# Two graph attention layers on one core: the first phase's pipeline is shortened by a step and put in another order

## The reference

```python
# graph attention, layer 0: h = x @ W; s1 = h @ a1; s2 = h @ a2
e = leaky_relu(s1[:, None] + s2[None, :], 0.2)
out0 = elu(softmax(where(adj > 0, e, NEG_INF), axis=1) @ h)
# attention, layer 1: q, k, v = x @ Wq.T + bq, x @ Wk.T + bk, x @ Wv.T + bv
scores = where(adj > 0, q @ k.T / sqrt(128), NEG_INF)
out1 = elu(softmax(scores, axis=-1) @ v)
# together
h = maximum(layernorm(x), 0); x = x + out0(h, adj)
h = maximum(layernorm(x), 0); x = x + out1(h, adj)
```

## Time and profile before

| what | us |
|---|---|
| median of 3 runs | 1703.05 (1699.79 to 1706.76) |
| the profiled execution, as timed | 1698.98 |
| its span in the profile | 1697.2 |
| DVE busy | 1220.4 (72%) |
| PE busy | 1195.3 (70%) |
| POOL busy | 1131.2 (67%) |
| ACT busy | 928.7 (55%) |

### The profile page before, as it was taken

How to read it: one execution, slowest core, us unless ns; L and a number is a source line. 1 busy time by engine, 2 the same in 40 slices (tenths; PEclk the granted TensorE clock), 3 DMA queues, 4 the chain that set the end, 5 groups by cost and what they waited for, 6 DMA issues and landing times.

```text
span 1697.2 us, 23466 instructions
## 1 busy us (share of the span) xinstructions
PE 1195.3 (70%) x5503; PEld 944.0 (56%) x5554; DVE 1220.4 (72%) x6625; ACT 928.7 (55%) x1891; POOL 1131.2 (67%) x1206
## 2 busy tenths in 40 slices
PE   2667877877877778777765566766776676767676
PEld 1344555555555555555545456665766666666665
DVE  3567888888888888888888366656665665566565
ACT  2769888888878878888852222332233323332322
POOL 1237766766766666666666477777777777777773
PEclk9878777777777778777775566567566666566665
DMA  9869999999999999999922122222222222222221
GB/s 293 347 238 394 399 401 400 392 384 378 378 385 380 385 381 386 369 388 386 378 59 56 50 58 57 66 65 65 64 66 66 65 63 66 64 66 64 66 65 41
DMA packets 113049, 368.10 MB, mean 217 GB/s; under 512 B 33553, under 2 KB 58642, under 8 KB 80146
## 3 DMA queue, kind: packets, MB, share of 16 engines
q1 hardware_dynamic: 66242, 285.50, 43.6%
q0 software_dynamic: 38464, 81.08, 17.4%
q10 hardware_dynamic: 8208, 0.03, 0.3%
HBM read 353.80 MB, written 12.72 MB: 216 GB/s over the span
## 4 chain that ended last, share of the span: by engine, by line
POOL 33%; DVE 27%; PE 20%; issue 13%; ACT 4%; DMA 2%; SPq 1%; POOLq 0%; ACTq 0%; DVEq 0%
POOL arena L598 32%; PE psum L1443 6%; PE psum L1429 4%; PE psum L1415 4%; ACT arena L1175 3%; PE psum L1382 3%; DVE arena L754 2%; DVE arena L757 2%; DMA table<-arena 1%; DVE arena L880 1%; DVE arena L864 1%; DVE arena L875 1%; DVE arena L892 1%; DVE arena L889 1%; DVE arena L827 1%
## 5 line engine op out<-in xcount | busy, mean ns | idle before, releaser
L568 POOL DMA_INDIRECT arena<-table,arena x576 | 553.8, 961 | 260.2 <-issue 160.6
L598 POOL DMA_INDIRECT arena<-table,arena x576 | 549.0, 953 | 184.0 <-issue 174.9
L1175 ACT ACTIVATE arena<-arena 128x2048 bf16<-128x2048 int32 x256 | 484.8, 1894 | 26.0 <-DMA arena<-in_adj_dram 26.0
L1382 PE MATMUL psum<-arena 128*128 128x512 bf16 x973 | 283.7, 428 | 51.5 <-ACT arena L1175 46.8
L864 DVE SCALAR_TENSOR_TENSOR arena<-arena 128x131 f32<-128x131 f32 (+1 forms) x768 | 267.0, 348 | 15.1
L1429 PE MATMUL psum<-arena 128*128 128x131 f32 (+1 forms) x768 | 200.6, 433 | 103.8 <-ACT arena L1317 102.1
L1415 PE MATMUL psum<-arena 128*128 128x18 f32 x768 | 145.1, 322 | 166.1 <-DVE arena L827 165.7
L1415 PEld LDWEIGHTS psum<-arena 128*128 128x128 f32 x768 | 138.4, 265 | 185.0 <-DVE arena L827 184.7
L1429 PEld LDWEIGHTS psum<-arena 128*128 128x128 f32 x768 | 179.1, 329 | 107.5 <-issue 107.5
L1382 PEld LDWEIGHTS psum<-arena 128*128 128x128 bf16 x1024 | 110.0, 116 | 189.0 <-issue 67.4
L1422 PE MATMUL psum<-arena 128*128 128x1 f32 x768 | 134.7, 291 | 108.0 <-DVE arena L847 108.0
(11 more groups left out here) (205 smaller groups left out, 2089.3 us busy)
## 6 DMA issues: line engine op xcount, KB each, us to landing
arena<-in_adj_dram SPq DMA_DIRECT2D x256, 1024.0 KB, 12.2
arena<-table,arena POOLq DMA_INDIRECT x1152
table<-arena POOLq DMA_DIRECT2D x32, 132.0 KB, 4.5
table<-arena SPq DMA_DIRECT2D x16, 256.0 KB, 9.6
arena<-table SPq DMA_DIRECT2D x64, 64.0 KB, 1.9
out_dram<-arena SPq DMA_DIRECT2D x16, 256.0 KB, 2.4
arena<-in_x_dram SPq DMA_DIRECT2D x4, 0.5 KB, 12.2
arena<-in_L_gnn_W_dram SPq DMA_DIRECT2D x1, 64.0 KB
```

The lines of the kernel that those rows point to most:

```text
L568: pool.indirect_dma_start(Gt[:, v % GROUP, c + 1, :], None, table0, bass.IndirectOffsetOnAxis(idx_now[:, v % GROUP, c:c + 1], 0))\
L598: pool.indirect_dma_start(Gt[:, t % GROUP, c + 1, 0:D], None, table1, bass.IndirectOffsetOnAxis(idx_now[:, t % GROUP, c:c + 1], 0))\
L1175: nc.scalar.activation(mask[:, k, q * QUARTER:(q + 1) * QUARTER], adj_sb[:, k, q, :], ACT.Relu, accum_out=sum_all[:, bass.ds(tile, 1), q:q ...
L1382: nc.tensor.matmul(V[k], shifted[:, s, :], mask[:, k, s * 512:(s + 1) * 512], start=(s == 0), stop=False)
```

## The change

- The lags fall by one step each: PICK 3 to 2, LATE 6 to 5, DONE 7 to 6, NORM 4 to 3, TURN 5 to 4.
- DVE: `decode`, both `list_tile` and `count` of a pair now stand at the end of the odd step. `split` goes from the odd to the even step, behind `weigh`. `mark` goes from ahead of the `extract` loop to behind its fifth part (MARK = 4). `pick` stands before `decode` and the rest, right behind `total`. `keep_self_turned` is gone.
- ACT: `measure_spans` goes behind quarter 1. ACT copies the turned own rows itself. `self_turned_ps` has two buffers instead of one. The root and stage work stands one step earlier.
- PE: `ends` comes behind `scatter` in the even step, and the deal goes from second place to behind the first half of `pack`. The projection waits for DVE's use of its target as well.
- The indices are written once, to `idx_all`; `idx_now`, its copy L820, `publish` (64 copies in the second phase) and POOL's second wait are gone.

```diff
-        ends_ps = bank(7)[:, 0:2]
+        ends_ps = bank(6)[:, 96:98]
-        self_turned_ps = bank(7)[:, 384:384 + P]
+        self_turned_ps = [bank(5 - k)[:, 256:256 + P] for k in range(2)]
...
-        PICK, LATE, DONE = 3, 6, 7
-        NORM, TURN = 4, 5
+        PICK, LATE, DONE = 2, 5, 6
+        NORM, TURN = 3, 4
...
 @@ POOL, second phase
                     pool.wait_ge(summed, T + t - 3)
-                    pool.wait_ge(idx_done, T + t + 1)
...
-                                                bass.IndirectOffsetOnAxis(idx_now[:, t % GROUP, c:c + 1], 0))\
+                                                bass.IndirectOffsetOnAxis(idx_all[:, t, c:c + 1], 0))\
...
 @@ DVE, pick
-                nc.vector.tensor_scalar(idx_now[:, b, :], dealt[:, b, LISTED:over + CHUNKS], 0.0, float(N), ALU.max, ALU.min)\
+                nc.vector.tensor_scalar(idx_all[:, v, :], dealt[:, b, LISTED:over + CHUNKS], 0.0, float(N), ALU.max, ALU.min)\
                   .then_inc(idx_done, 1)
-                dve.wait_ge(idx_done, v + 1)
-                nc.vector.tensor_copy(idx_all[:, at, :], idx_now[:, b:b + 1, :]).then_inc(pick_done, 1)
...
 @@ DVE, survey
-                    if b % 2 and live(t, 3):
-                        split(t - 3, (t - 3) % GROUP, (t - 3) // 2)
...
-                    if live(t, PICK):
-                        mark(v, v % GROUP)
+                    if b % 2 == 0 and live(t, PICK):
+                        split(v, v % GROUP, v // 2)
...
-                    if live(t, TURN):
-                        keep_self_turned(t - TURN)
+                        if n == MARK and live(t, PICK):
+                            mark(v, v % GROUP)
...
-                    if live(t, 1):
-                        pair = (t - 1) // 2
-                        if b % 2:
-                            decode(pair, pair % 2, t - 1)
-                        list_tile(t - 1, pair)
-                        if b % 2 == 0:
-                            count(t - 2, (t - 2) % GROUP, pair)
                     if live(t, PICK):
                         pick(v, v % GROUP)
...
-                    if b == 3 and 0 <= g - 2 < G:
+                    if b == 2 and 0 <= g - 2 < G:
                         polish(g - 2)
-                    if b == 2 and 0 <= g - 2 < G:
+                    if b == 1 and 0 <= g - 2 < G:
                         moments(g - 2)
+                    if b % 2 and live(t, 0):
+                        pair = t // 2
+                        decode(pair, pair % 2, t - 1)
+                        list_tile(t - 1, pair)
+                        list_tile(t, pair)
+                        count(t - 1, (t - 1) % GROUP, pair)
...
 @@ ACT, survey
+                    quarter(1)
                     if live(t, PICK):
                         act.wait_ge(split_done, 3 * (v // 2 + 1))
                         at_least(act, mine_done, v - 1)
                         measure_spans(v)
-                    quarter(1)
                     quarter(2)
...
+                    if live(t, TURN):
+                        o = t - TURN
+                        act.wait_ge(self_turned, o + 1)
+                        at_least(act, self_done, o)
+                        nc.scalar.activation(self_hT[:, :], self_turned_ps[o % 2], ACT.Identity).then_inc(self_hT_done, 1)
                     quarter(3)
...
 @@ PE, survey
                     if live(t, LATE):
                         scatter(u, u % 2, u % GROUP)
+                    if b % 2 == 0 and live(t, PICK):
+                        pe.wait_ge(count_done, 4 * (v // 2 + 1))
+                        nc.tensor.matmul(ends_ps, upto[:, :], over16[:, :], start=True, stop=True).then_inc(ends_done, 1)
+                    if live(t, DONE):
+                        at_least(pe, summed, w - 1)
+                        sum_up(w, w % 2, w % GROUP, D + 3)
+                    if live(t, TURN):
+                        o = t - TURN
...
+                        nc.tensor.transpose(self_turned_ps[o % 2], Gt[:, o % GROUP, 0, 0:D], ident[:, :]).then_inc(self_turned, 1)
+                    if live(t, -1):
...
+                        pack(t + 1, (b + 1) % 2, range(0, 8))
                     if live(t, PICK):
                         pe.wait_ge(mine_done, v + 1)
                         at_least(pe, owned_done, v - 1)
```

More of the change, by code:

```diff
@@ L39 @@
 DEALT = 155
+MARK = 4
 def two_layer_graph_attention(nc, x, adj, W, a, Wq, bq, Wk, bk, Wv, bv, out):
@@ L127, in two_layer_graph_attention @@
         hot = place([GROUP, CHUNKS, OVER])
-        idx_now = place([GROUP, ROWS - 1], U32)
         owned_list = place([GROUP, CHUNKS, DEALT])
@@ L475, in load_group @@
                             load_adj(s + 2, b % 2, q)
-                    if b == 2 and (not isinstance(g, int) or 0 <= g - 3 < G):
+                    if b == 1 and (not isinstance(g, int) or 0 <= g - 3 < G):
                         sp.wait_ge(stage_done, (g - 2) * GROUP)
@@ L568, in _ @@
                     pool.indirect_dma_start(Gt[:, v % GROUP, c + 1, :], None, table0,
-                                            bass.IndirectOffsetOnAxis(idx_now[:, v % GROUP, c:c + 1], 0))\
+                                            bass.IndirectOffsetOnAxis(idx_all[:, v, c:c + 1], 0))\
                         .then_inc(rows_in[v % GROUP], 16)
@@ L788, in mark @@
                   .then_inc(mine_done, 1)
-            PICK_STEPS = 6
+            PICK_STEPS = 5
             def pick(v, b):
@@ L1095, in _ @@
             with dve.Else():
-                def publish(t, b):
-                    nc.vector.tensor_copy(idx_now[:, b:b + 1, :], idx_all[:, bass.ds(t, 1), :]).then_inc(idx_done, 1)
                 def prepare(t, b):
@@ L1136, in attend @@
                         back, m = (b - 3) % GROUP, (b - 3) % 2
-                        if live(t, -1):
-                            publish(t + 1, (b + 1) % GROUP)
                         if live(t, 1):
@@ L1160, in _ @@
                 dve.wait_ge(dve_consts, DVE_CONSTS + 3)
-                publish(0, 0)
                 unrolled(attend, G + 1)
@@ L1252, in survey @@
                         nc.scalar.activation(m_root[:, :], m_root[:, :], ACT.Exp, scale=-0.5).then_inc(root_done, 1)
[L1253 to L1258, removed]
+                    f = g - 2 if b == 3 else g - 3
+                    if b in (0, 3) and 0 <= f < G:
+                        if b == 3:
+                            act.wait_ge(shift_done, f + 1)
+                            at_least(act, table1_in, 16 * f)
+                        for n in ((0, 1) if b == 3 else (2, 3)):
+                            nc.scalar.activation(stage[:, n:n + 1, :], X[:, bass.ds(f * GROUP + n, 1), :], ACT.Relu,
                                                  bias=m_shift[:, n:n + 1], scale=m_rstd[:, n:n + 1]).then_inc(stage_done, 1)
@@ L1438, in survey @@
                         scatter(u, u % 2, u % GROUP)
+                    if b % 2 == 0 and live(t, PICK):
[6 more added lines that the diff above has]
+                        o = t - TURN
+                        pe.wait_ge(self_h_done, o + 1)
+                        at_least(pe, summed, o - 2)
+                        nc.tensor.transpose(self_turned_ps[o % 2], Gt[:, o % GROUP, 0, 0:D], ident[:, :]).then_inc(self_turned, 1)
+                    if live(t, -1):
+                        at_least(pe, top_done, t)
+                        pack(t + 1, (b + 1) % 2, range(0, 8))
                     if live(t, PICK):
@@ L1445, in survey @@
                         last.then_inc(deal_done, 1)
[L1446 to L1457, removed]
                     if live(t, LATE):
@@ L1472, in survey @@
                         pe.wait_ge(self_hT_done, o + 1)
+                        if o >= 1:
+                            pe.wait_ge(e_done, 3 * (o - 1) + 1)
+                        if o >= 2:
+                            pe.wait_ge(chained, OWN * (o - 2) + 1)
                         nc.tensor.matmul(self_ps[o % 2], self_hT[:, :], ww[:, :], start=True, stop=True).then_inc(self_done, 1)
-                    if b % 2 == 0 and live(t, 2):
-                        pe.wait_ge(count_done, 4 * (t // 2))
-                        nc.tensor.matmul(ends_ps, upto[:, :], over16[:, :], start=True, stop=True).then_inc(ends_done, 1)
                     if t == T + 4:
```

3 lines of the change are left out of this document (removed).

## The result

The changed kernel took 1879.12 us (median of 4 runs, 1876.00 to 1887.29) against 1703.14 us (4 runs of the kernel before), a ratio of 1.104 (95% interval 1.0998 to 1.1082): slower. The profiled execution has a span of 1874.3 us against 1697.2, at a mean granted clock of 0.678. The forecast was 1830, the range 1690 to 1890; the measured time is inside it, 11 us from its upper edge.

The account below looks back on a forecast made before the run. It took DVE as the serial resource, with the loads' floor at 12.64 of 12.81 us a step. Steps of 15.2 us gave 58 x 2.4 = +139, less 9: +130 on 1699, 1833 with the offset, said as 1830; range 1690 to 1890.

Parts of the forecast that it names:

- The deal is a chain with no slack: First phase: PE's work ahead of the deal makes DVE and ACT wait; a step takes 15.2 us against 12.81.
- B = A + 12.3: From the start of ACT's deal copy in the even step (A) to the odd step's (B): 12.3 us.
- All other edits ... lie inside the wait of PE for quarter 3: 0: Turned-row buffers, projection's new waits and polish cost 0; without that cover, up to 1.7 us in one of four steps.
- The size of pick's wait: DVE in the even step: pick waits 3.0 us for ACT's deal copy, with the split's wait for the ends inside.
- "-9" for the saved step: Start of the first phase: the shorter pipeline saves one light step, -9 us.
- The clock as the lever: PE in the first phase: longer waits pull more of its chain to the low clock, towards a bound of 16.0 us.
- The floor of the loads, 12.64: First phase: loads need an estimated 12.64 us a step, so a faster pipeline gains at most 0.17 us a step.
- Transition and second phase, 0: POOL's first gather and the second phase: from 0 to -8.7 us at the start, 0 taken; gathers unchanged at 1.25 us.
- Relief of DVE wins: Rival, first phase: DVE's own work falls to 11.8 us a step, loads bound it; -19 us, 1684; chance 0.12.

Follow-up runs that it names:

- The projection ahead: The changed kernel with PE's projection before the last four matmuls of pack: 1849.8 us, ratio 1.0876 to the kernel before.
- six moves: The changed kernel with quarter 3, deal, ends, projection and spread_max earlier on their queues, and decode between total and pick: 1679.9 us, ratio 0.9867 to the kernel before.
- a filler: The changed kernel with 32 matmuls of 240 columns that nothing reads, ahead of PE's scatter in even steps: 1847.2 us, ratio 1.0868 to the kernel before.
- indices only in the list: The kernel before with the gathers' indices written once, to the layer's list, and no copy of them: 1693.4 us, ratio 0.9954.
- ACT copies the turned rows: The kernel before with only the copy of the turned own rows moved from DVE to ACT: 1685.8 us, ratio 0.9911.

## Why the prediction was right, and where it was off

The cause is shown: it is the order on the queues, with the low clock behind its waits as a part of the price. The change puts PE's deal behind work that was behind it, and ACT's quarter 3, PE's pack and projection and DVE's scores hang on it in a ring. Another order alone, with the lags and the rest of the change kept, takes 199 us off and makes the kernel faster than before. The forecast had that mechanism, and came out 47 us low.

- *The deal is a chain with no slack.* Right. The deal's copy starts on average 8.0 us after an even step's start (8.2 said; 7.48 in the pair shown). From there to the odd step's copy it takes 13.7 (12.3 said), from it to the next even start 9.9 (9.95 said, with the whole moments block of 0.25 in every pair, though it comes in every other one). The four steps of a group take 10.3, 21.4, 13.3 and 18.4 on average: even 11.8 (11.0 said), odd 19.9 (19.4 said).
- *The term that was too small: B = A + 12.3, since "All other edits ... lie inside the wait of PE for quarter 3: 0".* It measured 13.7. In the pair shown PE is free at 457.1, 6.2 us after the deal's copy, as said. But scatter starts 1.05 us later, since the scores wait for the projection (L830, 3.51 us) and PE then for the scores: 30 us over 29 pairs. "The projection ahead" measured 29 us for that wait. The scatter-to-deal stretch was 5.4 for 4.83. Polish waited 1.6 us for ACT's root in every fourth step (20.7 us in all), of the size said, but costed at 0.
- *The size of pick's wait.* It is the first of DVE's, as said. 3.0 us said in the even step, 1.15 in the pair shown (2.2 on average over both kinds): the split in front of it waited 1.1 us for the ends, which I had put inside, and DVE arrived later. The copy's time, which sets the end, came out nearly right, so it moved little.
- *"-9" for the saved step.* Its size is luck. It was taken from the light steps at the start, and came as -8.5 at the end of the phase, where the pipeline runs empty. The start is 15.9 us longer instead; the sum has 2.4 for each of the three full steps outside the 55, 7 in all. With 55 steps of 0.69 more than said, 38, that makes 15.9 - 7 + 38 + 0.5 = 47, the distance from the forecast span (1697.2 + 130) to the measured one. The start's 15.9 us stand almost wholly in one step, t = 5, which the sum still has as a light one: it takes 22.4 us (137.8 to 160.2) against 9.35 before. With the lags shortened the first scores come in this step, a step earlier, while POOL's first gather starts no earlier (at 127.95 us, 126.25 before). DVE waits in it 5.88 us for gathered rows, which the kernel before does not, and then 5.45 us for the deal's copy. With six moves the ninth tile still starts 7 us later than before (161.2): there the wait for gathered rows is 5.4 us and pick's is 0.9. So the deal's part went with the order; that the rest comes with the shorter pipeline is read from these traces, and no run tried it alone.
- *The clock as the lever.* Right in kind: 0.50 behind PE's long wait, 0.72 over the phase against 0.77, and a filler returns 32 us.
- *The floor of the loads, 12.64.* Nearly: three kernels in which ACT waits for loads have 12.53, 12.57 and 12.59. Relief of DVE alone was worth more than the 0.17 us a step allowed, 0.28 (12.81 to 12.53).
- *Transition and second phase, 0.* Right: "indices only in the list" leaves the idle time of 8.73 untouched, and a gather takes 1.25 us. A DMA share of 0.83 was said, 0.84 came; loads land in 6.4 us (under 8 said).
- *Relief of DVE wins.* The rival's relief exists, with its size: the two parts on the kernel before give 1686 and 1693, and its 1684 is near what the six moves reach (1679.9). It was overrun by the order. What went from DVE there was 0.21 us of work a step and the wait of 0.86. The Trainium skill's advice to work on the engine with the highest occupancy first (Perfetto Trace Analysis, Identifying the Most-Contended Engine) agrees with "ACT copies the turned rows" (-14.7); with the whole change, which relieves the same engine and costs 176 us, it doesn't.

Not settled: what the low clock costs in all, and how much the ends' and decode's moves do by themselves; neither was run alone. Nor was the change run with the old lags: that the shorter pipeline does no harm is shown only together with the new order.

## What to carry to other kernels

When instructions are moved on in-order queues, follow the moved result through every engine until it comes back to the first: if the walk closes into a ring, its length is the step, whatever the busy shares say. Of the waits of this ring the cheapest to cut was the one where work that depends on nothing in the ring (a quarter of the mask) was queued behind an instruction that waits; look for that first. Try the parts of a change singly: two of these gained 0.9% and 0.5%, the first already at the loads' floor, and the order hid them behind a loss of 10%. A shorter pipeline can also have a price at its start: here the first scores came a step earlier, and met gathers that had not landed.

## What the runs showed of the hardware

- The loads' floor is sharp: steps of 12.53, 12.57 and 12.59 us in three kernels (two with the old order, one with a new one), with DMA shares of 1.00 to 1.01 and 387 to 388 GB/s in the window view. A share of 1.00 without any wait for a load, as in the earlier trace rows, went with a floor 2% away (12.81 against 12.53).
- 5.06 us of matmuls that nothing reads, ahead of the chain, made the kernel 32 us faster. In the step shown, scatter and the sums behind them took 0.84 and 0.92 us instead of 1.47 and 1.66, at a granted clock of 1.00 (432.9 to 440 us) where the changed kernel had 0.50.
- ACT's copy of 128x128 from PSUM took 0.26 us, near the 0.29 of DVE's, and quarter 3 started 0.16 us behind it (452.53 to 452.69): in this place one more small copy held ACT up for less than its row says.
